# The MLP of a two-layer kernel: its thresholds searched two chunks at a time, and another start of the attention stage

## The reference

```python
# attention: two score maps, one softmax over their difference
qkv = x @ W_attn
attn1 = jnp.einsum('bthd,bshd->bhts', q1, k1) * scale
attn2 = jnp.einsum('bthd,bshd->bhts', q2, k2) * scale
score = jax.nn.softmax(attn1 - lam * attn2, axis=-1)
out = (1.0 - LAMBDA_INIT) * einsum('bhts,bshd->bthd', score, v)
x = x + out @ W_proj
# MLP: ternary weights, the top 102 of 1024 units kept in each row
def ternary_quant(W):
    scale = jnp.mean(jnp.abs(W))
    return jnp.clip(jnp.round(W / (scale + 1e-08)), -1.0, 1.0) * scale
z = x_flat @ ternary_quant(W_syn).T + b_syn
thresh = jax.lax.top_k(z, k)[0][:, -1:]         # k = 102
hidden = jnp.where(z >= thresh, jax.nn.relu(z), 0.0)
out = hidden @ ternary_quant(W_out).T + b_out
x = x + layernorm(xn + out, gamma, beta)        # xn: the block's normalised input
```

## Time and profile before

| | us |
|---|---|
| median of 3 runs | 1280.05 (1278.74 to 1283.57) |
| profiled execution, its own time | 1277.8 |
| its span, first to last instruction | 1276.0 |
| attention, first "max" unit to last output | about 64.4 to 463.2 |
| MLP, first transpose to last add | 463.5 to 725.5 |
| granted TensorE clock, mean | 0.899 |

### The profile page before, as it was taken

One profiled execution on the slowest core, in us unless ns is written; L12 is line 12 of the kernel. 1 busy time (PEld: TensorE's weight loads), 2 busy tenths in 40 slices (PEclk: granted clock), 3 DMA queues, 4 the chain that ended last, 5 costly groups with the idle time before them and its releaser, 6 DMA issues. The chain is left out here.

```text
span 1276.0 us, 17985 instructions
## 1 busy us (share of the span) xinstructions
PE 1071.7 (84%) x6832; PEld 739.1 (58%) x6832; DVE 904.3 (71%) x1697; ACT 630.3 (49%) x1097; POOL 212.1 (17%) x172
## 2 busy tenths in 40 slices
PE   3959999999999866665757559999997899999798
PEld 2823333333333235554646448888885799899696
DVE  7687899999999324589888576555554777877733
ACT  2514778888788853676631123333334333433233
POOL 5008000000000001000033203000001644744100
PEclk9955899999999997777878779999997999999859
DMA  2872032033110010000000200110100000000200
GB/s 101 232 188 45 7 52 47 6 51 51 30 24 3 2 38 1 0 1 1 1 1 1 61 26 33 34 34 17 34 1 33 2 1 1 1 1 1 88 1 5
DMA packets 24848, 39.99 MB, mean 31 GB/s; under 512 B 3116, under 2 KB 12344, under 8 KB 24760
## 3 DMA queue, kind: packets, MB, share of 16 engines
q1 hardware_dynamic: 24760, 38.82, 12.5%
HBM read 28.06 MB, written 10.49 MB: 30 GB/s over the span
## 5 line engine op out<-in xcount | busy, mean ns | idle before, releaser
L660 DVE TENSOR_REDUCE att_mx<-att_ps_m 128x2 f32<-128x1024 f32 x256 | 310.2, 1224 | 36.8 <-PE att_ps_m L559 32.7
L643 ACT ACTIVATE att_prob<-att_ps_s 128x512 f32<-128x512 f32 x512 | 278.3, 596 | 81.8 <-PE att_ps_s L585 72.4
L601 PE MATMUL att_ps_o<-att_prob,v_rows 128*32 128x256 f32 (+1 forms) x1920 | 165.5, 419 | 4.6 <-ACT att_osb L651 4.6
L585 PE MATMUL att_ps_s<-qst,kst 50*128 50x512 f32 x512 | 132.9, 515 | 11.4 <-ACT att_prob L643 10.2
L1703 POOL TENSOR_TENSOR qry_prod<-qry_qr,lin_ksum 128x512 f32<-128x512 f32 x64 | 88.0, 1376 | 307.1 <-ACT qry_qr L1770 307.1
L559 PE MATMUL att_ps_m<-kst,qst 48*128 48x512 f32 x512 | 116.3, 452 | 12.5 <-DVE att_mx L660 11.2
L585 PEld LDWEIGHTS att_ps_s<-qst,kst 50*128 50x128 f32 x512 | 49.9, 190 | 125.8 <-ACT att_prob L643 115.2
L1770 ACT ACTIVATE qry_qr<-qry_ps_q 128x512 f32<-128x512 f32 x64 | 38.3, 598 | 129.8 <-PE qry_ps_q L152 116.4
L1446 DVE SCALAR_TENSOR_TENSOR key_k_lo<-key_ps_k,key_k_hi 128x512 fp32r<-128x512 f32 x64 | 44.2, 691 | 67.8 <-ACT key_k_hi L1526 67.3
L601 PEld LDWEIGHTS att_ps_o<-att_prob,v_rows 128*32 128x32 f32 x1920 | 39.1, 109 | 89.6 <-ACT att_prob L643 67.3
L1058 ACT ACTIVATE mlp_junk<-mlp_z,mlp_nlev 128x1024 bf16<-128x1024 f32 x64 | 72.7, 1139 | 23.0 <-DVE mlp_nlev L894 21.4
(11 more groups left out here) (342 smaller groups left out, 2388.1 us busy)
## 6 DMA issues: line engine op xcount, KB each, us to landing
qst<-qk_parts SPq DMA_DIRECT2D x48, 128.0 KB, 4.1
kst<-qk_parts SPq DMA_DIRECT2D x48, 128.0 KB, 5.9
qk_parts<-att_out SPq DMA_DIRECT2D x16, 256.0 KB, 4.6
qk_parts<-qk_lo SPq DMA_DIRECT2D x16, 256.0 KB, 4.7
residual<-L_attn_x SPq DMA_DIRECT2D x4, 512.0 KB, 5.7
lin_wq_raw<-L_attn_Wk SPq DMA_DIRECT2D x4, 512.0 KB, 3.5
lin_wq_raw<-L_attn_Wv SPq DMA_DIRECT2D x4, 512.0 KB, 3.4
lin_wq_raw<-L_attn_Wq SPq DMA_DIRECT2D x4, 512.0 KB, 5.9
```

The source lines that it names most:

```text
L585: ins = nc.tensor.matmul(ps_s[:, (n + r) % BANKS, :], kst[g % RING][rows, j, s * P:(s + 1) * P], qst[g % RING][rows, t, j, :], start=True, ...
L601: ins = nc.tensor.matmul(ps_o[32 * h:32 * h + 32, cols], vall[:, NS * b + s, h0 + h, :], prob[:, u % PR, h, cols], start=s == 0, stop=s == ...
L643: nc.scalar.activation(prob[:, u % PR, 2 * j + r, :], ps_s[:, (n + r) % BANKS, :], ACT.Exp).then_inc(exp_ok, 1)
L660: nc.vector.reduce_max(mx[:, v % 2, :, m], ps_m[:, n % 2], AX.X).then_inc(m_rd, 1)
```

## The change

The diff is cut to its core. Of the attention stage: the weight sum becomes a side unit "sum" of step 2, with its scaling on VectorE instead of ScalarE and its place in the two banks `ps_m`; the wait for `sc_ok` ahead of the first score goes; SP issues the loads of W_syn and W_out ahead of those of group 1; eight matmuls `keep_busy`, whose result nobody reads, follow the last eight units of the prologue; and the value matmuls of the first step of each row of keys are issued behind the second score pair of their step, not behind the first.

Of the MLP: the skewed steps are replaced by one written order on each engine. A batch b is two chunks (BT = 8 tiles), and a search round counts and moves the levels of eight tiles at once; round 0 is counted in two halves, each as soon as its chunk has its first level. All four chunks enter before the first one's threshold is taken; then all four leave. The slots of `ps_z` are given to all z tiles first, then to all hidden tiles. Output tiles alternate over two banks of `ps_p` and two of `ps_t` in every chunk, where before the two of `ps_t` served only the last chunk. GpSimd adds b_out for all chunks before it works on y. `high`, `low`, `turn`, `expand`, `eight`, `threshold`, `settle`, `hidden`, `closing` and `closed` work as before.

```diff
-        SUM_AT = 20
+        SUM_AT = 2
...
+        side[SUM_AT].append(("sum", 0, 0))
...
-                slot = 2 * (u + LAG) + (0 if u % NS == 0 else c)
+                slot = 2 * (u + LAG) + (1 if u % NS == 0 else c)
...
-                load_group(1)
                 for i, name in enumerate(("W_syn", "W_out")):
                     sp.dma_start(w_raw[:, i, :].rearrange("p (a n) -> p a n", n=d.E if i == 0 else d.N),
                                  io["L0_ffn_" + name].rearrange("(a p) n -> p a n", p=P)).then_inc(wt_in[i], 16)
+                load_group(1)
...
-                pool.wait_ge(sc_ok, 1)
+                pool.wait_ge(m_rd, place("sum", 0))
...
+                    elif kind == "sum":
+                        pe.wait_ge(ones_ok, 1)
+                        pe.wait_ge(sum_ok, 2)
+                        ins = nc.tensor.matmul(ps_m[:, n % 2, 0, 0:2], ones[:], abs_sum[:], start=True, stop=True)
...
-                    if n == 0:
-                        pe.wait_ge(sc_ok, 1)
-                    else:
+                    if n:
                         pe.wait_ge(exp_ok, n + 2 - BANKS)
...
-                def weight_sum():
-                    pe.wait_ge(ones_ok, 1)
-                    pe.wait_ge(sum_ok, 2)
-                    nc.tensor.matmul(ps_s[:, 0, 0:2], ones[:], abs_sum[:], start=True, stop=True).then_inc(sum_ps, 1)
+                def keep_busy(k):
+                    nc.tensor.matmul(ps_s[:, k % BANKS, :], ones[:], vall[:, k, :, :].rearrange("p h e -> p (h e)"),
+                                     start=True, stop=True)
+                pe.wait_ge(ones_ok, 1)
                 for n, x in enumerate(side[-1]):
                     side_unit(*x)
-                    if n == SUM_AT:
-                        weight_sum()
+                    if n > HM + 2:
+                        keep_busy(n - HM - 3)
...
-                act.wait_ge(sum_ps, 1)
-                nc.scalar.activation(sc[:], ps_s[:, 0, 0:2], ACT.Copy, scale=1.0 / (d.N * d.E)).then_inc(sc_ok, 1)
+                act.wait_ge(sum_ok, 2)
...
+                    elif kind == "sum":
+                        nc.vector.tensor_scalar(sc[:], ps_m[:, n % 2, 0, 0:2], 1.0 / (d.N * d.E), None, ALU.mult)\
+                            .then_inc(m_rd, 1)
...
-        DEPTH = 4
+        BT = 2 * TPC
+        LEVELS = 2 + ROUNDS - 1
...
-        t1, t2, t3, msk = (st.sb(n, [P, TPC]) for n in ("t1", "t2", "t3", "msk"))
+        t1, t2, t3, msk = (st.sb(n, [P, BT]) for n in ("t1", "t2", "t3", "msk"))
...
+        ring = [(kind, t) for kind in ("z", "h") for t in range(d.NT)]
...
-            last_two = t // TPC + DEPTH - 1 >= d.NC and t % TPC >= 2
-            return (ps_t if last_two else ps_p)[:, t % 2, 0:d.E]
+            return (ps_p if t % TPC < 2 else ps_t)[:, t % 2, 0:d.E]
...
+                for c in range(d.NC):
+                    pool.wait_ge(t_ps, d.KT * (c + 1))
+                    for j in range(TPC):
+                        t = TPC * c + j
+                        ins = nc.gpsimd.tensor_tensor(XN[:, t, :], XN[:, t, :], vecs[:, 0, :], ALU.add)
+                    ins.then_inc(xb_ok, 1)
+                for c in range(d.NC - 1):
+                    pool.wait_ge(y_ok, c + 1)
...
-                def next_level(c, r):
-                    cs = slice(TPC * c, TPC * (c + 1))
+                def next_level(b, r):
+                    cs = slice(BT * b, BT * (b + 1))
                     LEV, CNT = lev[:, cs], cnt[:, cs]
-                    dve.wait_ge(cnt_ok, TPC * (ROUNDS * c + r + 1))
+                    dve.wait_ge(cnt_ok, BT * (ROUNDS * b + r + 1))
...
+                def spread_chunk(c):
+                    for j in range(TPC):
+                        ins = spread(TPC * c + j)
+                    link(ins)
+                    spreads(c)
...
-                for s in range(d.NC + DEPTH):
-                    enter, count, settles, leave = steps(s)
-                    if enter is not None:
-                        normal(enter)
-                    if leave is not None:
-                        hidden(TPC * leave)
-                        hidden(TPC * leave + 1)
-                    if count is not None:
-                        next_level(count, 0)
-                    if enter is not None:
-                        low(enter)
-                    if leave is not None:
-                        hidden(TPC * leave + 2)
-                        hidden(TPC * leave + 3)
...
+                normal(0)
+                low(0)
+                dve.wait_ge(bs_h, 1)
+                nc.vector.tensor_tensor(bs_lo[:], below[:, 0, :], as_f32(bs_hi[:]), ALU.subtract).then_inc(bs_ok, 1)
+                dve.wait_ge(on, 1)
+                link(nc.vector.tensor_copy(iota8[:], iota_i[:]))
+                residual(1)
+                normal(1)
+                spread_chunk(0)
+                low(1)
+                first_level(0)
+                residual(2)
+                spread_chunk(1)
+                normal(2)
+                first_level(1)
+                low(2)
+                next_level(0, 0)
+                residual(3)
+                spread(TPC * 2)
+                link(spread(TPC * 2 + 1))
+                next_level(0, 1)
+                normal(3)
+                spread(TPC * 2 + 2)
+                link(spread(TPC * 2 + 3))
+                spreads(2)
+                low(3)
+                next_level(0, 2)
+                first_level(2)
+                spread_chunk(3)
+                first_level(3)
+                next_level(0, 3)
+                eight(0, (0, 1))
+                eight(0, (2, 3))
+                threshold(0)
+                next_level(1, 0)
+                eight(1, (0, 1))
+                settle(0)
+                hide(0)
+                eight(1, (2, 3))
+                next_level(1, 1)
+                threshold(1)
+                outputs(0)
+                closing(0)
+                settle(1)
+                hide(1)
+                next_level(1, 2)
+                closed(0)
+                outputs(1)
+                closing(1)
+                next_level(1, 3)
+                closed(1)
+                eight(2, (0, 1))
+                eight(2, (2, 3))
+                threshold(2)
+                eight(3, (0, 1))
+                settle(2)
+                hide(2)
+                eight(3, (2, 3))
+                threshold(3)
+                outputs(2)
+                settle(3)
+                hide(3)
+                closing(2)
+                closed(2)
+                outputs(3)
+                closing(3)
+                closed(3)
...
+                def counts(b, r, js):
+                    act.wait_ge(lev_ok, LEVELS * b + (1 + js[0] // TPC if r == 0 else r + 2))
...
-                for s in range(d.NC + DEPTH - 1):
-                    enter, count, _, leave = steps(s)
...
+                def root(c):
+                    act.wait_ge(zvar, c + 1)
+                    nc.scalar.activation(zsd[:, TPC * c:TPC * (c + 1)], zmv[:, :, 1], ACT.Sqrt).then_inc(zroot, 1)
+                def evacuate(kind, c, js):
+                    for j in js:
+                        evacuate_one(kind, TPC * c + j)
+                first, second, every = range(TPC), range(TPC, BT), range(BT)
+                high(0)
+                evacuate("z", 0, (0, 1))
+                attended(1)
+                turned_out(0)
+                evacuate("z", 0, (2, 3))
+                norm_root(nc, act, w1, 2)
+                turned_out(1)
+                root(0)
+                high(1)
+                counts(0, 0, first)
+                evacuate("z", 1, (0, 1))
+                attended(2)
+                evacuate("z", 1, (2, 3))
+                norm_root(nc, act, w1, 3)
+                root(1)
+                counts(0, 0, second)
+                high(2)
+                evacuate("z", 2, (0, 1))
+                counts(0, 1, every)
+                attended(3)
+                evacuate("z", 2, (2, 3))
+                norm_root(nc, act, w1, 4)
+                counts(0, 2, every)
+                root(2)
+                high(3)
+                evacuate("z", 3, (0, 1))
+                evacuate("z", 3, (2, 3))
+                counts(0, 3, every)
+                root(3)
+                counts(1, 0, first)
+                counts(1, 0, second)
+                counts(1, 1, every)
+                evacuate("h", 0, (0, 1))
+                evacuate("h", 0, (2, 3))
+                counts(1, 2, first)
+                evacuate("h", 1, (0, 1))
+                counts(1, 2, second)
+                evacuate("h", 1, (2, 3))
+                norm_root(nc, act, w2, 1)
+                counts(1, 3, every)
+                norm_root(nc, act, w2, 2)
+                evacuate("h", 2, (0, 1))
+                evacuate("h", 2, (2, 3))
+                evacuate("h", 3, (0, 1))
+                evacuate("h", 3, (2, 3))
+                norm_root(nc, act, w2, 3)
```

(59 more changed lines are left out.)

196 lines of the change are left out of this document (38 added, 158 removed).

## The result

The changed kernel took 1314.95 us (median of 5 runs, 1310.32 to 1329.65) against 1280.05 us before: ratio 1.0293, 95% interval 1.0246 to 1.034. Slower, by 35 us; 1304 (1291 to 1322) was forecast.

What follows compares the result with a forecast made beforehand. No one engine was taken to bound the kernel; queue order and waits set the MLP, and a low TensorE clock marked the prologue. 1277.8 - 13 - 1 + 38.5 = 1302.3, plus 2.25 for the median: 1304 us, range 1291 to 1322.

Steps and rivals of the forecast that it cites:

- the forecast's own case: Whole kernel: MLP longer and attention prologue at the high clock, 1293 to 1312 us, chance 0.65.
- The large term: MLP: chunk entries wait behind ScalarE's blocks of counts and thresholds begin only after all entries, +38.5 us.
- the forecast's own bounds: MLP: +18 us with every tail wait halved, +50 with TensorE cold through projects 1 and 2 and first reduces.
- The mis-sized term: Attention prologue: clock rises near 91 us and holds, step 9 at 122.2 instead of 135.4, gain 13 us.
- the two prologue terms: Attention: 13 us gained by the high clock and 1 us by the value group moved one half-step later.
- the value group moved one half-step later: Attention, each new row of keys: 0.1 us over 15 boundaries, 1 us of gain, between -3 and +1.
- the second rival: Attention prologue stays at or falls back to the low clock, MLP as forecast: 1317 to 1322 us, chance 0.20.
- The rival of the other sign: MLP: ScalarE's blocks of counts hide, 31.6 us go from the entry, kernel at 1272 us, chance 0.07.
- Four banks worth nothing: MLP outputs: four output banks gain nothing, since reduces wait for hidden tiles, not for banks.
- the forecast's walk of the tail: MLP after the last entry: item-by-item timing from 614.9 to 764 us, with 41 us of waits.
- the fourth rival: MLP: transposes do not raise the clock, three leaves' first reduces start cold, 2 us each, 1310 us, chance 0.04.

Runs made afterwards that it cites:

- experiment 2: The kernel before with the new MLP alone, prologue as it was: 1312.7 us against 1278.6, stage 281.5 us.
- the warm base: The changed kernel plus an early exponential table load and extra 128-column matmuls in the prologue's first two units: 1303.0 us.
- experiment 4: The kernel before with the new prologue and two additions, early exponential table load and 128-column matmuls in the first two units: 1264.45 us, ratio 0.9887.
- experiment 3: The changed kernel with chunk entry work moved ahead of blocks of counts in the ScalarE and VectorE queues: 1310.0 us.
- (6): The warm base with the first batch's last round and chunk 0's threshold moved into chunk 3's entry: 1307.3 us, 4.3 more than that base.
- (9): The warm base with chunk 3's entry and the search rounds drawn forward together, counts split in halves: 1285.5 us, 17.5 less than that base.
- (8): The warm base with the second batch's levels and counts moved ahead of work for chunks 0 and 1: 1311.5 us, 8.5 more than that base.

## Why the prediction was right, and where it was not

**The sum.** 1304 was forecast and 1315 measured: inside the whole range of 1291 to 1322, but above the 1293 to 1312 of the forecast's own case, whose condition (the prologue at the high clock) did not come about. The large term came out. MLP: +38.5 forecast; measured +34.1 with the old prologue (experiment 2), +38.5 with the warm one (1303.0 against 1264.5), +39.7 in the changed kernel's own trace. The entry times held in that trace: 31.6, 32.2 and 45.2 us apart against 31.6, 32.2 and 45.3. VectorE's longest wait is that for project(3), 23.0 us; it is busy 106.4 us behind the first `eight()` where 108 was worked out, and 167.2 us in a stage of 303.3 (from 470.7 on) where 171 in 302 were. The mechanism is right; that it agrees to a tenth is luck, since the forecast's own bounds were +18 and +50 and on the warm base the same entries lie 30.2, 31.4 and 44.6 us apart.

**The mis-sized term: the prologue, -13.** It measured -6.5 alone (1272.1 against 1278.6), where -14 was the sum of the two prologue terms; the value group moved one half-step later, -1, was not measured apart. The rise came where it was placed. The step that failed is that it holds: the first half-steps, busy "some 0.9 of 1.26 us", were compared to 4.4 of 8 us in a later stretch and found enough. They were not: the clock fell at 104.7 to 105.7 in every profile without the extra matmuls but with keep_busy. Two smaller misses stand beside it. A unit and its keep_busy took 1.48 us, not 1.2, and the scores start at 100.81, not 98.2. And the forecast has no term for the table load of the exponential, which the change moves behind the wait for the scores. The change takes away the scaling ahead of it on ScalarE and puts a second wait there; which of its edits moved the load was not tested apart. With the clock held (experiment 4) the gain is 14.1 us in time and 14.6 in the trace, where 13 + 1 were forecast, but step 9 is reached 11.7 us sooner and not 13.2; the rest came later in the stage.

In the profiled run the second rival was the one that happened, and at a higher price than it had: a clock that rises and falls again was counted as no loss, and in this run the MLP starts to expand 7.7 us later than in the earlier trace rows. From parts the changed kernel should take 1280 - 6.5 + 38.5 = 1312. Its five runs, from 1310 to 1330, have granted clocks of 0.893, 0.893, 0.892, 0.888 and 0.880 in order of time, which fits cold stretches of different length; only the longest run was profiled.

**The MLP's reason was half right.** The forecast named the blocks of counts ahead of attended(3), high(3) and root(3), and it named the thresholds that begin only when all has entered. The first without the second is nothing (experiment 3), and the second bought with a later entry is a loss (6). VectorE's idle time shows the whole: ahead of 134 us 38.7 before and 80.9 on the warm base, behind it 27.3 and 42.7. That is 57.6 us more idle, less 20.7 us of work saved (178.7 to 158.0): 36.9, the difference of the two stages. In the old order most of the waits of an entry were filled with an older chunk's `eight()`, hidden rows and outputs; in the new one these come after. Drawing entry and rounds forward together (9) gives back 17.5 us. The remaining 21 are read as the price of an order in which VectorE has 105 us of work, with waits between, behind the first `eight()`. That no order inside this second part does better is not shown; the one that was tried (8) did worse.

**The rival of the other sign** gave 31.6 us to hidden blocks of counts. The closest to it that was built gave 17.5; it was not near.

**Four banks worth nothing** was wrong for the new order, by 13.4 us. It was argued from the old order, where outputs follow their reduces by pairs. The sum did not suffer, since the forecast's walk of the tail never let a reduce wait for a bank.

**Transposes and the clock** (the fourth rival): on the warm base the first reduce behind a pair of turnings took 4.78 us and the next 3.62, so that one began cold. In the other three leaves the first reduce took 3.63, 3.67 and 3.98 us. So a pair of turnings raises the clock nearly in time in most leaves, and the rival's price of 2 us in each of three was not paid. The timeline of TensorE on that base:
```profile
645.43 3.65 PE L1231 MATMUL mlp_ps_z<-ident,mlp_hid 128*128 128x128 f32 x16 [4.39 <-DVE mlp_hid L950]
...
648.87 4.78 PE L1245 MATMUL mlp_ps_p<-mlp_wo_t,mlp_ht 128*128 128x256 f32 x16
...
654.36 3.62 PE L1245 MATMUL mlp_ps_p<-mlp_wo_t,mlp_ht 128*128 128x256 f32 x16
...
698.89 3.67 PE L1245 MATMUL mlp_ps_p<-mlp_wo_t,mlp_ht 128*128 128x256 f32 x16
...
722.17 3.98 PE L1245 MATMUL mlp_ps_p<-mlp_wo_t,mlp_ht 128*128 128x256 f32 x16
```
Before the change four tiles were turned ahead of the first reduce, which ran at full clock; now two are. Whether the kind of matmul or only the length of the dense work decides was not tested apart.

## What to carry to other kernels

When a queue is rewritten so that all chunks enter before the first leaves, add up the idle time of the engine with most work in the old entry, and ask what filled it: that filling is the price. Moving one wait away is worth nothing if the same engine's next item waits for the same source; walk two items further before claiming a gain. And work that raises the clock needs work that holds it until the dense part begins, and a look at what used to hide behind the wait that was removed.

## What was not expected of the hardware

The granted clock fell to 0.50 at 104.7 to 105.7 us, behind a window (100 to 104) in which TensorE was busy 1.74 to 2.64 of 4 us. In one run it then stayed there through 40 us in which TensorE was busy for 39.67; in another run of the same prologue it came back after some 13 us. The matmuls of that stretch use 48 or 50 rows, or 32 columns four at a time; which of their traits keeps it low was not tested. The Trainium skill, "TensorE: Matmul & The Clock Gate", Part 1, says that the number of cold matmuls differs from run to run of one kernel; the spread of these runs agrees (1266.3 us at a granted clock of 0.914 to 1280.3 at 0.900 in one kernel). It also puts the cost of the ramp below 1% of a usual kernel; here the two additions that hold the clock are worth 7.6 of 1272.1 us, 0.6%, and the whole new prologue with them 14.1 of 1278.6, 1.1%.

The load of a table took 1.28 us in the changed kernel's profile as in that before. The Trainium skill, "ScalarE: Activation LUTs", What ACT_TABLE_LOAD costs, has the same figure for the load (about 1283 ns), and adds a drain of about 1380 ns for each switch of tables. No such drain shows here: in the changed kernel the exponential starts at 102.69, 0.02 us behind the load's end. What the load cost differs with its place: TensorE waited 1.80 us instead of 0.45 in the changed kernel, and not at all before.
